# Attention's score pass for row maxima moved half a head group further ahead, on three PSUM banks; projections and transposes on one bank

## The reference

```python
x = _layernorm(x + _L0_attn_ref(x, ...))            # a linear recurrence, a gate and an MLP
x = _layernorm(x + _L0_xattn_ref(x, ctx, ctx, ...)) # the attention below
x = _layernorm(x + _L0_ffn_ref(x, ...))             # 48 experts, each takes its top 64 tokens

# attention: 16 heads of 16 dims, 512 tokens, causal
Q, K, V = proj(query, wq_w, wq_b), proj(key, wk_w, wk_b), proj(value, wv_w, wv_b)
scores = jnp.einsum('bhqd,bhkd->bhqk', Q, K) * scale
scores = jnp.where(causal, scores, -jnp.inf)
attn = jax.nn.softmax(scores, axis=-1)
out = jnp.einsum('bhqk,bhkd->bhqd', attn, V)
```

## Time and profile before

| | |
|---|---|
| runs | median 815.03 us of 3 (811.88 to 816.0) |
| profiled execution | 816.48 us; span of its instructions 814.7 us; mean granted clock of PE 0.884 |
| PE busy | 612.5 us (75% of the span) |
| DVE, ACT, POOL busy | 358.4, 274.5, 195.1 us (44%, 34%, 24%) |
| attention loop, one trip (329.2 to 411.1) | 81.9 us, PE busy 65.06 |
| its groups 1, 2, 3, 0 | 27.7, 14.7, 13.0, 26.5 us |

### The profile page before, as it was taken

How to read it: one execution, slowest core, us unless ns; L and a number is a source line. 1 busy time by engine, 2 the same in 40 slices (tenths; PEclk the granted TensorE clock), 3 DMA queues, 4 the chain that set the end, 5 groups by cost and what they waited for, 6 DMA issues and landing times.

```text
span 814.7 us, 12126 instructions
## 1 busy us (share of the span) xinstructions
PE 612.5 (75%) x3942; PEld 351.0 (43%) x3942; DVE 358.4 (44%) x777; ACT 274.5 (34%) x458; POOL 195.1 (24%) x253
## 2 busy tenths in 40 slices
PE   3599999999467877787778788760089979789930
PEld 2458585847133445344534454340035535445520
DVE  3633533322564555455635564329823323223315
ACT  2141514141025463546354636510033322223304
POOL 1242221210051211021102111200032233335324
PEclk9899999999569899989998989965589999898965
DMA  6840000003410341134113334018159999994247
GB/s 229 299 162 1 0 0 0 25 27 108 138 40 1 113 140 45 40 116 135 38 46 114 109 114 179 1 53 338 84 176 372 408 387 326 315 378 88 35 98 231
DMA packets 53618, 112.25 MB, mean 138 GB/s; under 512 B 5920, under 2 KB 44496, under 8 KB 50512
## 3 DMA queue, kind: packets, MB, share of 16 engines
q1 hardware_dynamic: 48272, 105.06, 35.8%
q0 software_dynamic: 4608, 6.29, 4.1%
q10 hardware_dynamic: 704, 0.47, 0.2%
HBM read 91.88 MB, written 17.83 MB: 135 GB/s over the span
## 4 chain that ended last, share of the span: by engine, by line
PE 49%; DMA 16%; DVE 15%; issue 9%; ACT 7%; POOL 3%; SPq 1%; ACTq 0%; DVEq 0%; POOLq 0%
DMA sums<-row 9%; PE PS L1451 7%; PE PS L1442 7%; DMA sums<-wo_s,row 4%; DVE Mx L991 4%; PE PS L1730 4%; PE PS L1526 4%; PE PS L1610 3%; PE PS L1597 3%; PE PS L1567 3%; PE PS L1518 2%; PE PS L1413 2%; PE PS L1430 2%; PE PS L1563 2%; PE PS L1545 2%
## 5 line engine op out<-in xcount | busy, mean ns | idle before, releaser
L991 DVE TENSOR_REDUCE Mx<-PS 128x1 f32<-128x384 f32 (+3 forms) x176 | 107.3, 638 | 85.4 <-PE PS L1567 83.7
L1292 ACT ACTIVATE arena<-PS 128x512 f32<-128x512 f32 (+1 forms) x176 | 86.0, 565 | 87.6 <-PE PS L1597 87.6
L711 POOL TENSOR_SCALAR_AFFINE_SELECT arena<-arena 128x512 f32<-128x512 f32 x64 | 40.8, 638 | 217.9 <-ACT arena L1292 217.9
L1597 PE MATMUL PS<-arena 99*128 99x512 bf16 (+3 forms) x256 | 55.8, 307 | 26.3 <-ACT arena L1279 12.6
L1563 PE MATMUL PS<-causal,identb 128*128 128x128 bf16 (+2 forms) x176 | 45.8, 260 | 34.0 <-DVE Mx L991 24.7
L1567 PE MATMUL PS<-arena 96*128 96x128 bf16 (+3 forms) x256 | 68.1, 322 | 0.0
L1147 DVE TENSOR_TENSOR X<-PS,Y 128x512 f32<-128x512 f32 x48 | 31.4, 688 | 66.7 <-PE PS L1743 66.4
L1442 PE MATMUL PS<-arena 128*128 128x512 f32 x128 | 55.8, 593 | 1.6 <-issue 1.6
L1451 PE MATMUL PS<-arena 128*128 128x256 f32 x256 | 55.9, 379 | 0.0
L1359 ACT ACTIVATE X<-X 128x512 f32<-128x512 f32 x48 | 29.6, 632 | 71.3 <-DVE X L1147 68.1
L1610 PE MATMUL PS<-arena 128*32 128x128 f32 (+3 forms) x512 | 52.3, 481 | 1.0 <-POOL arena L711 0.9
(11 more groups left out here) (183 smaller groups left out, 997.6 us busy)
## 6 DMA issues: line engine op xcount, KB each, us to landing
ring_a<-experts SPq DMA_DIRECT2D x12, 2048.0 KB, 10.2
arena<-experts SPq DMA_DIRECT2D x12, 2048.0 KB, 10.3
arena<-pieces SPq DMA_DIRECT2D x192, 64.0 KB, 2.3
ring_a<-experts SPq DMA_DIRECT2D x12, 512.0 KB, 4.8
arena<-experts SPq DMA_DIRECT2D x12, 512.0 KB, 7.4
pieces<-arena SPq DMA_DIRECT2D x4, 768.0 KB, 3.7
pieces<-ring_a SPq DMA_DIRECT2D x4, 768.0 KB, 3.7
X<-x SPq DMA_DIRECT2D x4, 512.0 KB, 3.6
```

Of the source, the lines that this page charges most:

```text
L711: pool.affine_select(out=pb[j % 2][:, :, 0:P], in_=pb[j % 2][:, :, 0:P], compare_op=ALU.is_ge, fill=0.0, base=0, pattern=[[0, GH], [1, P]] ...
L991: dve.tensor_reduce(Mx[:, g % 2, i, heads[0]:heads[-1] + 1], bank((g * NSH + u) % 2)[:, 0:len(heads) * w] .rearrange("p (h n) -> p h n", h ...
L1292: act.activation(pb[j % 2][:, heads[0]:heads[-1] + 1, 0:w], bank(2 + n % 3)[:, 0:len(heads) * w] .rearrange("p (h n) -> p h n", h=len(heads)),
L1597: mm = pe.matmul(bank(2 + n % 3)[:, a * w:(a + 1) * w], KTs[0:SX, g * GH + h, j * P:(j + 1) * P], QTs[0:SX, g * GH + h, j * P:T], start=Tr ...
```

## The change

1. Score banks run in the order of tiles 3, 2, 0, 1 (`TILE_ORDER`), on three banks (0, 1, 5) by turns, so PE waits for the reduce three banks back. In slots 2 and 3 they belong to the group after the next (tiles 3 and 2), in slot 0 to the next (tiles 0 and 1), in slot 1 there are none (`AHEAD`, `TILES_OF`).
2. `negate` moves to slot 0, `minus_max` to slot 1, of the group before the one it serves.
3. Everything that took bank 5 or 7 takes bank 7.
4. `PREPARE`'s steps move up: both halves of `key` and `query_in` 0 in slot 0, `query_in` 1, `split_k`, `query` 0 in slot 1, `query` 1 and `split_q` in slot 2. Value 0 moves behind the score banks of its slot.
5. The weights of queries and keys are permuted on the host, so that a partition's four heads lie in one run; `group_in` issues three DMAs instead of six for each side, of 48, 32 and 16 partitions, with the repeated piece broadcast.
6. POOL sets the ones rows before the root of the last norm. DVE takes the statistics of that norm after `negate` and runs two tiles of group 1's maxima before it applies the norm; PE issues those score banks before the first slot.
7. `project(1)` stands ahead of `turn_2(0)`. DVE takes the first statistics before the phase and applies the norm before its two long parts.
8. `shifted` waits for each half of the negated maxima where it first needs it.

The diff, cut (left out: the passing of the new argument `scored` through ACT's and POOL's slots, the renaming of `SCORED` to `SHARES` in them, and the host's weight arrays beside the helper shown):

```diff
@@ -29,9 +29,9 @@
...
 SX = SK + NPC
-K_PIECES = (0, 1, 2, 0, 1, 0)
-Q_PIECES = (0, 0, 0, 1, 1, 2)
-NRD = 2 * NPR
+K_RUNS = ((0, 1, 3), (0, 1, 2), (0, 1, 1))
+Q_RUNS = ((0, 0, 3), (1, 0, 2), (2, 0, 1))
+NRD = len(K_RUNS) + len(Q_RUNS)
 VW = 32
@@ -49,32 +49,39 @@
...
 NSH = 11
+LAST_IN_BANK = [max(n + 1 for n in range(NG * NSH) if n % 3 == u) for u in range(3)]
...
-TILES_OF = [(0, 1), (2,), (3,), ()]
-CUTS = [(2, 3), (2, 3), (0, 4), (0, 0)]
+TILE_ORDER = (3, 2, 0, 1)
+STARTS = [sum(len(SHARED_Q[t]) for t in TILE_ORDER[:n]) for n in range(TT)]
+SCORED = {i: list(zip([i] * NSH, range(start, NSH), SHARED_Q[i]))
+          for i, start in zip(TILE_ORDER, STARTS)}
+TILES_OF = [(0, 1), (), (3,), (2,)]
+AHEAD = (1, 1, 2, 2)
+CUTS = [(3, 3), (0, 0), (2, 3), (2, 3)]
 def _cut(tiles, cuts):
-    banks = [(i, n, heads) for i in tiles
-             for n, heads in enumerate(SHARED_Q[i], sum(len(q) for q in SHARED_Q[:i]))]
+    banks = [bank for i in tiles for bank in SCORED[i]]
     return banks[:cuts[0]], banks[cuts[0]:cuts[1]], banks[cuts[1]:]
-SCORED = [_cut(tiles, cuts) for tiles, cuts in zip(TILES_OF, CUTS)]
+SHARES = [_cut(tiles, cuts) for tiles, cuts in zip(TILES_OF, CUTS)]
 PREPARE = {
-    (1, 0): ([("query_in", 0)], [], [("query_in", 1)]),
-    (1, 1): ([("key", 0)], [("key", 1)], [("query", 0)]),
-    (1, 2): ([("split_k", 0)], [("query", 1)], []),
-    (1, 3): ([("split_q", 0)], [], []),
-    (2, 1): ([], [("value", 0)], []),
+    (1, 0): ([("key", 0)], [("key", 1)], [("query_in", 0)]),
+    (1, 1): ([("query_in", 1)], [("split_k", 0)], [("query", 0)]),
+    (1, 2): ([("query", 1)], [], [("split_q", 0)]),
+    (2, 1): ([], [], [("value", 0)]),
 }
@@ -438,7 +446,11 @@
...
                 prev = None if first else (c, g - 1) if g > 0 else (b, NG - 1)
-                then = None if last and g == NG - 1 else (c, g + 1) if g + 1 < NG else (c + 1, 0)
+                ahead = [None] + [(c, g + n) if g + n < NG else (c + 1, g + n - NG)
+                                  for n in (1, 2)]
+                for n in (1, 2):
+                    if last and g + n >= NG:
+                        ahead[n] = None
                 for j in range(TT):
@@ -531,12 +543,18 @@
...
                 heads = slice(GH * g, GH * g + GH)
-                rows_g = slice(GH * HD * (g % 2), GH * HD * (g % 2) + GH * HD)
-                for n, (dst, order) in enumerate(((KTs, K_PIECES), (QTs, Q_PIECES))):
-                    for r, c in enumerate(order):
-                        sp.dma_start(dst[HD * r:HD * r + HD, heads, :],
-                                     pieces[n, c, g // 2, rows_g, :]
-                                     .rearrange("(h d) t -> d h t", d=HD)).then_inc(kq_in[g].s, 16)
+                at = GH * (g % 2)
+                for n, (dst, runs) in enumerate(((KTs, K_RUNS), (QTs, Q_RUNS))):
+                    first = 0
+                    for c, step, count in runs:
+                        part = pieces[n, c:c + (count if step else 1), g // 2]\
+                            .rearrange("c (d h) t -> c d h t", d=HD)[:, :, at:at + GH, :]\
+                            .rearrange("c d h t -> c d (h t)")
+                        if not step:
+                            part = part.to_broadcast([count, HD, GH * T])
+                        sp.dma_start(dst[first:first + HD * count, heads, :]
+                                     .rearrange("p h t -> p (h t)"), part).then_inc(kq_in[g].s, 16)
+                        first += HD * count
@@ -690,6 +708,11 @@
...
             pool.memset(Vb[:, :, :, HD:HD + 1], 1.0).then_inc(vset, 1)
+            pool.wait_ge(vset, 2)
+            pool.wait_ge(m2.s, m2.now(B - 1, 1))
+            for g in range(NG):
+                pool.memset(KTs[SK:SX, GH * g:GH * g + GH, :], 1.0).then_inc(ones, 1)
+            pool.wait_ge(ones, NG)
             root(ln3, rs3, B - 1, 1 + 2 * TT)
@@ -718,10 +741,6 @@
...
-            pool.wait_ge(m2.s, m2.now(B - 1, 1))
-            for g in range(NG):
-                pool.memset(KTs[SK:SX, GH * g:GH * g + GH, :], 1.0).then_inc(ones, 1)
-            pool.wait_ge(ones, NG)
             with_bias(0)
@@ -843,11 +862,14 @@
...
+            dve.wait_ge(x_in.s, x_in.now(0, 1))
+            statistics(ln1, X, 0, 0, 0)
             dve.wait_ge(consts, CONSTS)
...
             link(dve.tensor_scalar(ph, ph, vec[:, V_FRQ:V_FRQ + 1], None, ALU.mult))
-            for turn, dst in ((0.0, rot[:, 0:C]), (0.25, rot[:, C:2 * C])):
+            def phase(turn, dst):
@@ -856,7 +878,10 @@
...
                 link(dve.tensor_scalar(dst, ph_m, -3.1415925, None, ALU.max))
-            ln_in(0)
+            norm(ln1, rs1, X, lambda t: xn1[:, t, :], 0, 0, (xt1.s, xt1.before(0, 1)))
+            phase(0.0, rot[:, 0:C])
+            phase(0.25, rot[:, C:2 * C])
             dve.wait_ge(trig, 3)
@@ -989,7 +1014,7 @@
...
                     dve.tensor_reduce(Mx[:, g % 2, i, heads[0]:heads[-1] + 1],
-                                      bank((g * NSH + u) % 2)[:, 0:len(heads) * w]
+                                      bank(score_banks[(g * NSH + u) % 3])[:, 0:len(heads) * w]
                                       .rearrange("p (h n) -> p h n", h=len(heads)),
@@ -1050,28 +1075,31 @@
...
-            def dve_slot(b, g, j, prev, then, *steps):
-                shares = SCORED[j] if then is not None else ([], [], [])
-                maxima(then, shares[0])
+            def dve_slot(b, g, j, prev, then, scored, *steps):
+                shares = SHARES[j] if scored is not None else ([], [], [])
+                maxima(scored, shares[0])
                 if j == 0 and prev is not None:
...
                 dve_do(steps[0])
-                maxima(then, shares[1])
+                maxima(scored, shares[1])
                 dve_do(steps[1])
-                maxima(then, shares[2])
-                if j == 2 and then is not None:
+                maxima(scored, shares[2])
+                if j == 0 and then is not None:
                     negate(*then)
...
             ln_out(B - 1)
-            spare_banks[:] = 5, 7
-            for share in SCORED:
-                for banks in share:
-                    maxima((0, 0), banks)
+            spare_banks[:] = 7, 7
+            for i in TILE_ORDER:
+                maxima((0, 0), SCORED[i])
             negate(0, 0)
-            ln_out_norm(B - 1)
+            dve.wait_ge(ln3.s, ln3.now(B - 1, 1))
+            statistics(ln3, X, (B - 1) * TT, B - 1, 1)
+            for i in TILE_ORDER[:2]:
+                maxima((0, 1), SCORED[i])
+            norm(ln3, rs3, X, lambda t: X[:, (B - 1) * TT + t, :], (B - 1) * TT, B - 1)
             slots(0, dve_slot, first=True)
@@ -1467,8 +1495,8 @@
...
             turn(ln1, xt1, xn1, 1, 4, (xe1.s, xe1.now(0, KT)))
+            project(1)
             turn_2(0)
-            project(1)
             pe.wait_ge(w_mlp, 32)
@@ -1490,14 +1518,15 @@
...
-            read_by = {0: None, 1: None}
+            read_by = {}
...
-                if read_by[k % 2] is not None:
-                    pe.wait_ge(*read_by[k % 2])
-                read_by[k % 2] = (sig.s, value)
+                at = spare_banks[k % 2]
+                if read_by.get(at) is not None:
+                    pe.wait_ge(*read_by[at])
+                read_by[at] = (sig.s, value)
                 return spare(k)
@@ -1555,11 +1584,11 @@
...
-                    if u >= 2 or g > 0:
-                        pe.wait_ge(mxs.s, mxs.now(b, NSH * g + u - 1))
+                    if u >= 3 or g > 0:
+                        pe.wait_ge(mxs.s, mxs.now(b, NSH * g + u - 2))
                     else:
-                        pe.wait_ge(mxs.s, mxs.before(b, NSH * NG + u - 1))
-                    o = bank((g * NSH + u) % 2)
+                        pe.wait_ge(mxs.s, mxs.before(b, LAST_IN_BANK[u]))
+                    o = bank(score_banks[(g * NSH + u) % 3])
                     pe.matmul(o[:, 0:len(heads) * w].rearrange("p (h n) -> p h n", h=len(heads))
@@ -1583,9 +1612,9 @@
...
                 w = T - j * P
-                if j == 0:
-                    pe.wait_ge(nte.s, nte.now(b, 2 * g + 2))
                 for n, heads in enumerate(SHARED[j], FIRST[j]):
+                    if j == 0 and heads[0] % 2 == 0:
+                        pe.wait_ge(nte.s, nte.now(b, 2 * g + heads[0] // 2 + 1))
@@ -1649,54 +1678,54 @@
...
-            def pe_slot(b, g, j, prev, then, *steps):
-                shares = SCORED[j] if then is not None else ([], [], [])
+            def pe_slot(b, g, j, prev, then, scored, *steps):
+                shares = SHARES[j] if scored is not None else ([], [], [])
                 for n, _ in enumerate(shifted(b, g, j)):
                     of = len(SHARED[j])
-                    scores(then, shares[0][n * len(shares[0]) // of:
+                    scores(scored, shares[0][n * len(shares[0]) // of:
                                            (n + 1) * len(shares[0]) // of])
...
                 pe_do(steps[0])
-                scores(then, shares[1])
```

(28 more changed lines are left out.)

19 lines of the change are left out of this document (10 added, 9 removed).

## The result

The changed kernel takes **879.31 us** (872.82 to 887.67), the kernel before 813.45 (810.2 to 816.0) on the same chip: ratio **1.0776**, 95% interval 1.0719 to 1.0832. Here and in some experiments one run had a lower granted clock and took longer (here 887.67); medians and ranges hold it, ratios leave it out. The forecast, slower at 822, had the sign and a small part of the size; 879 lies far outside 805 to 834. The profiled execution took 879.33, with a span of 877.6.

The account below looks back on a forecast made before the run. PE, busy 75% of the span, was taken as the bound. Start -1.0, swap -3.8, attention set-up -8.0, trips +19.2, last batch -2.0 and tail +2.5 sum to +6.9: 816.48 to 823.4, forecast 822 as median, range 805 to 834.

Parts of the forecast that it names:

- The step that failed first: loads: Set-up of attention: six loads leave after 2.9 us, land 2.3 later, at 207.7; later groups' loads over 2 us in hand.
- The second step: the trips: Three trips of the attention loop: +6.4 us each, +19.2 together, from waits and half clock.
- The walk at full clock: One attention-loop trip at full clock: group 1 +0.4, group 2 -0.1, group 3 -0.6, group 0 +2.8, together +2.5 us.
- The clock: Half clock after PE pauses: group 1 +2.5 us (bounds 0 to 6.2), group 0 +1.4 (0 to 4.3), per trip.
- Rival (a): Attention loop: the clock stays at full through short pauses; three trips cost +7.5, time 811.7, median 810; chance 0.27.
- Rival (c): Attention loop: half clock reaches every group through slot 1's pause; twelve groups outside group 1 lose 1.0 us, 834; chance 0.10.
- Start: Kernel start: DVE takes statistics before the sine preparation; transposes near 9 instead of 12.44, -1.0 us.
- The swap: `project(1)` before `turn_2(0)`, ahead of the first expand: expand from 45.0 instead of 48.77, -3.8 us.
- Rival (b): Attention groups: waits put behind each other overlap; 1.3 us gone in each of 16 groups, 21 us, time 802; chance 0.13.
- A third score bank: Attention scores: it keeps DVE from holding PE for single matmuls but does not raise DVE's own pace.
- The last batch: Group 2 has no scores in slots 2 and 3: 11.1 instead of 12.9; others -0.2; together -2.0 us.
- The tail's three waits: Kernel's end: heads, output and turn each wait once for the bank's evacuation, 0.75 + 0.9 + 0.85 = +2.5 us.

Follow-up runs that it names:

- e1: The changed kernel with each merged load split again into loads of 16 partitions, twelve per group; permuted weights stay: 847.04 us.
- e14: The twelve-load changed kernel with dummy matmuls filling PE's pauses in groups 1 and 0, more of them in group 0 than in e6: 831.35 us.
- e2: The kernel before with only the rearranged weights and the six merged loads: 832.89 us.
- e6: e1 with dummy bf16 matmuls filling PE's pauses in groups 1 and 0: 833.64 us.
- e3: The kernel before with three small moves: statistics ahead of the sine phases, `project(1)` ahead of `turn_2(0)`, memsets ahead of the last root: 800.27 us, ratio 0.9838.
- e4: e1 with bank 5 given back: scores on banks 0 and 1, everything else on 5 and 7: 804.36 us.
- e11: e3 with projections and transposes of attention sharing bank 7, order and look-ahead of before, bank 5 unused: 838.32 us.
- e12: e1 without the third score bank: scores alternate banks 0 and 1, bank 5 unused, bank 7 shared: 866.28 us.
- e13: e4 with the batch's finish moved, pauses in group 0's slot 3 filled (eight dummies ahead of the wait), and e7's layout and nine loads: 784.82 us, ratio 0.9683.
- e7: The changed kernel with pieces laid out so merged key-side loads have 48, 32 or 16 outermost; query side six loads of 16 partitions: 849.36 us.

## Why the prediction was right in sign and wrong in size

Groups of a trip in us; the measured ones are those of one trip of each profile:

| group | forecast | changed kernel | e1, twelve loads | e14, clock full |
|---|---|---|---|---|
| 1 | 30.6 | 30.6 | 30.6 | 29.1 |
| 2 | 14.6 | 24.7 | 16.5 | 14.9 |
| 3 | 12.4 | 14.0 | 12.5 | 12.5 |
| 0 | 30.7 | 36.5 | 35.5 | 30.9 |
| trip | 88.3 | 105.7 | 95.1 | 87.4 |

- **The step that failed first: loads.** "Six leave after 2.9, landing 2.3 later: 207.7", and "loads for group g still have over 2 us in hand". The issues cost 3.5 us and the last load took 10.1. I priced a merged load by its issue and its bytes, with landing times of loads of another shape in the earlier trace rows, and gave the unknown no bound above; that the new access pattern began with a dimension of 2 or 3 stood in the diff. It cost 32 of the 66 us (e1), 21 on its own (e2). No rival covered it. From its first score bank on, the set-up went as walked: 15.5 us to the first shifted matmul, in the changed kernel (207.94 to 223.46) and in e1 (203.19 to 218.71), forecast 15.4. That both points of e1 lie near the forecast 202.9 (207.7 less 4.8) and 218.3 is luck: its MLP stage ended 6.5 us earlier, not 4.8, and its wait for loads stayed at 7.55 us, where six quick loads were to leave 5.6.
- **The second step: the trips.** With twelve loads the kernel still takes 847.04, above the range. Its three trips cost 44.0 us more than before (288.9 against 245.0) for a forecast of 19.2. Of that 27 is clock, forecast 11.7 (e1 less e14), and 17 is waits at full clock, forecast 7.5 (e14 less before): both terms were less than half of what they measured.
- **The walk at full clock had the waits, and was short.** Its groups, 28.1, 14.6, 12.4 and 29.3, came to 29.1, 14.9, 12.5 and 30.9 in e14: 84.4 forecast, 87.35 measured, so +5.5 over the 81.9 where +2.5 was forecast (what the fills cost is inside it). Outputs 0 and 1 are 7.5 us apart (424.75 and 432.23), over the 5.5 asked for. Group 0 was 1.6 short: in e14 output 0 came 9.6 us into the group, as walked, output 1 at 16.2 for 15.5, and what follows it took 12.9 for 12.0, with 0.99 us in it in which PE waits for a reduce.
- **The clock was mis-sized.** 3.9 a trip, of it 1.4 in group 0 with bounds 0 to 4.3; the fills show 7.7 in the middle trip and 9.0 on average, 4.6 to 5.6 of it in group 0 (35.5 to 36.5 in e1, 30.9 in e14). I had bounded only output 1, turns and logits; value 1 (3.32 for 1.95) and the values behind the transposes, which follow pauses of 1.15, 0.69 and 1.11 us, were left out. In group 1 the sign that I had named came: from 360 to 367, in slot 1, the clock was 0.66. Rival (a), the clock stays up, was wrong. Rival (c), the half clock in every group, was partly right: in the trips of e1 group 2 took 14.9 to 16.5 us and group 3 12.5 to 14.1, in e14 always 14.9 and 12.5, so some of them lost the 1 us or more that (c) put on each, and others nothing.
- **Start.** The transposes came at 8.79, near 9 as forecast, and the projection behind them 1.4 us earlier than before (14.70 for 16.12), for a forecast 1.0. The rest is clock: the projection took 3.67 us for 4.80, and `mix(0)` 3.69 from 24.68 for 5.38 from 27.22, so that it ended 4.2 earlier. The swap gave 4.0 (forecast 3.8). First expand at 40.43, before at 48.61 (the prediction has 48.77), so 8.2 earlier for a forecast 4.8. Part of that is luck of the profiled execution: with the same code in this stretch e6 has its first expand at 40.43 too, but e1, e3, e4, e11, e12 and e13 at 42.0 to 42.3, e14 at 44.64 and e7 at 45.18.

```profile
24.68 3.69 PE L1458 MATMUL PS<-arena 128*128 128x256 f32 x16 [2.85 <-POOL arena L677]
...
40.43 10.13 PE L1470 MATMUL PS<-arena 128*128 128x512 f32 x23 [1.62 <-ACT arena L1235]
```

- **Rival (b)**, the look-ahead is worth more than the walk says: not in this kernel. With two spare banks it holds for groups 1 and 3, 23.0 and 12.2 us in e13 (27.6 and 13.0 before), and not for groups 2 and 0.
- **A third score bank** "does not raise DVE's own pace": true, and beside the point. It kept DVE fed, 19 us (e12), which the walk had taken for granted.
- **The last batch** was to give 2.0: its group 2 took 12.9 instead of the forecast 11.1, and 11.3 in e14. The tail's three waits for the shared bank came as named (heads 0.78, output 0.88, turn 0.78): +3.2 for +2.5.

Open: how much of the 5.5 us of waits at full clock belongs to each shared use, and whether the fills cost anything inside a trip; neither was tried. That fills would win back the longer busy time of the shared bank in the old order (e11) was not tried either, nor were fills in the order of before.

## What to carry to other kernels

Before merging transfers, read the outermost dimension of both access patterns: here fewer, larger loads with 2 or 3 in front ran at a DMA share of 0.1 to 0.2, and a change of layout that put 16 to 48 there loaded four groups in 17.1 us, less than the 22.4 of twelve small loads a group. A spare PSUM bank was worth more where two engines must read a result in turn before it is free (62 us) than as a third bank for scores (19); count the evacuation on PE's path, and then, as the upper bound, the matmuls that follow such pauses at half clock, all of them. Where PE must pause anyway, cheap matmuls into a free bank, placed ahead of the wait and not behind it, can pay for themselves.
